# Attention kernel on one core: another table of steps, and the second fill of ones and three reads moved in the prologue

## The reference

```python
# layer 0 and 1: group norm, then attention with 8 heads of 16 channels
xn  = group_norm(x); q, k, v = split(xn @ w_qkv)          # per image: 1024 tokens
out = softmax(q k^T / sqrt(16)) v                         # per head, 1024 x 1024
h0  = out @ w_out + b_out + x                             # layer 0
h1  = out @ w_out + b_out + xn                            # layer 1
# layer 2: layer norm, layer 3: group norm; one head of 128 channels
out = softmax(q k^T / sqrt(128)) v @ Wp + bp + x
```

## Time and profile before

| what | value |
|---|---|
| median of three runs | 2097.07 us (2094.5 to 2097.71) |
| profiled execution: time, span | 2098.85 us, 2097.1 us |
| PE busy | 2034.3 us, 97% |
| PE weight loads | 1147.0 us, 55% |
| DVE busy | 1676.5 us, 80% |
| ACT busy | 1490.4 us, 71% |
| POOL busy | 413.9 us, 20% |
| tile maxima on DVE (line 1227) | 2048, 1271.1 us |
| exponentials on ACT (line 1117) | 2048, 1060.4 us |
| values on PE (line 1473) | 3080 products of 512 columns, 2032 of 256 |

### The profile page before, as it was taken

One profiled execution on the slowest core, in us unless ns is written; L12 is line 12 of the kernel. 1 busy time (PEld: TensorE's weight loads), 2 busy tenths in 40 slices (PEclk: granted clock), 3 DMA queues, 4 the chain that ended last, 5 costly groups with the idle time before them and its releaser, 6 DMA issues.

```text
span 2097.1 us, 40849 instructions
## 1 busy us (share of the span) xinstructions
PE 2034.3 (97%) x15800; PEld 1147.0 (55%) x15800; DVE 1676.5 (80%) x3104; ACT 1490.4 (71%) x2722; POOL 413.9 (20%) x544
## 2 busy tenths in 40 slices
PE   4799999999999999999999999999999999999999
PEld 3344444444744468444873448644585446846988
DVE  6799999999799978898789876898878977773433
ACT  1387788888588854988569874698747986597555
POOL 5002021220122311113120221203111031031231
PEclk7799999999999999999999999999999999999999
DMA  5401351412041314031230502305031040000000
GB/s 148 92 12 40 74 102 31 83 55 49 29 84 39 65 31 81 12 77 27 56 67 2 102 2 57 66 2 102 2 87 27 2 99 4 7 7 2 11 1 21
DMA packets 48592, 97.42 MB, mean 46 GB/s; under 512 B 7824, under 2 KB 10640, under 8 KB 48272
## 3 DMA queue, kind: packets, MB, share of 16 engines
q1 hardware_dynamic: 48400, 94.81, 21.1%
HBM read 55.98 MB, written 37.75 MB: 45 GB/s over the span
## 4 chain that ended last, share of the span: by engine, by line
PE 82%; DVE 10%; DMA 3%; ACT 2%; issue 2%; SPq 1%; POOL 1%; POOLq 0%; DVEq 0%; ACTq 0%
PE outs L1473 19%; PE banks L1435 14%; PE banks L1448 12%; PE outs L1513 11%; PE banks L1491 9%; DVE part_max L1227 8%; PE banks L1354 7%; PE banks L1360 5%; PE banks L1363 4%; ACT probs L1117 2%; DMA q_stack<-shift_parts 2%; SPq L904 0%; DMA q_scratch<-parts 0%; DVE o_turn L1239 0%; DVE stats L1166 0%
## 5 line engine op out<-in xcount | busy, mean ns | idle before, releaser
L1227 DVE TENSOR_REDUCE part_max<-banks 128x1 f32<-128x512 f32 x2048 | 1271.1, 680 | 166.6 <-PE banks L1435 161.4
L1117 ACT ACTIVATE probs<-banks 128x512 f32<-128x512 f32 x2048 | 1060.4, 611 | 200.0 <-PE banks L1448 172.8
L1473 PE MATMUL outs<-probs,v_heads 128*32 128x512 f32 (+1 forms) x5112 | 563.6, 522 | 0.8
L1435 PE MATMUL banks<-k_stack,q_stack 62*128 62x512 f32 x2048 | 550.9, 443 | 4.0 <-DVE part_max L1227 1.3
L1448 PE MATMUL banks<-q_stack,k_stack 64*128 64x512 f32 x2048 | 519.1, 444 | 21.4 <-DMA q_stack<-shift_parts 20.5
L1435 PEld LDWEIGHTS banks<-k_stack,q_stack 62*128 62x128 f32 x2048 | 257.4, 187 | 282.3 <-DVE part_max L1227 114.9
L1448 PEld LDWEIGHTS banks<-q_stack,k_stack 64*128 64x128 f32 x2048 | 244.0, 186 | 236.5 <-ACT probs L1117 77.2
L1124 ACT ACTIVATE probs<-banks,neg_max 128x1024 f32<-128x1024 f32 x128 | 142.7, 1115 | 220.9 <-DVE neg_max L1259 184.7
L1513 PEld LDWEIGHTS outs<-v_full,probs 128*128 128x128 f32 x2048 | 257.4, 191 | 47.0 <-issue 37.2
L1513 PE MATMUL outs<-v_full,probs 128*128 128x128 f32 x2048 | 276.8, 279 | 0.0
L1259 DVE TENSOR_REDUCE neg_max<-banks 128x1 f32<-128x1024 f32 x128 | 156.3, 1223 | 134.0 <-PE banks L1491 133.0
(11 more groups left out here) (107 smaller groups left out, 1160.3 us busy)
## 6 DMA issues: line engine op xcount, KB each, us to landing
k_scratch<-parts SPq DMA_DIRECT2D x64, 256.0 KB
q_scratch<-parts SPq DMA_DIRECT2D x64, 256.0 KB
k_stack<-k_scratch SPq DMA_DIRECT2D x64, 256.0 KB, 6.9
q_stack<-q_scratch SPq DMA_DIRECT2D x64, 256.0 KB, 8.2
k_stack<-k_scratch SPq DMA_DIRECT2D x64, 128.0 KB, 8.2
q_stack<-q_scratch SPq DMA_DIRECT2D x64, 128.0 KB, 9.7
q_stack<-shift_parts SPq DMA_DIRECT2D x256, 4.0 KB
tmp<-x SPq DMA_DIRECT2D x7, 512.0 KB, 3.3
```

Source lines behind the costliest of these rows:

```text
L1117: nc.scalar.activation(probs[:, plan.prob[u], 2 * n + half, :], banks[:, plan.banks["pair", t][k], :], ACT.Exp, scale=HEAD_SCALE).then_inc ...
L1227: nc.vector.tensor_reduce(part_max[:, r % 2, column:column + 1], bank_of(("tile", r, n)), AX_X, ALU.max, negate=True).then_inc(tile_max, 1)
L1435: nc.tensor.matmul(bank_of(("tile", r, n)), qs[rows, i, a, heads, P * t:P * (t + 1)], ks[rows, i, keys, heads, :], start=True, stop=True). ...
L1473: last = nc.tensor.matmul(outs[2 * HD * n:2 * HD * (n + 1), columns], v_heads[:, i, key, at:at + 2 * HD], probs[:, plan.prob[u], n, column ...
```

## The change

Three edits.

1. `STEPS`, the table behind the first 40 tiles, is another string. Both have the same number of T, P, H, S, R, G and Y. The old one has 385 V and 254 U, the new one 433 V and 158 U, so 48 slots whose values were in halves are now in one. Two V with nothing of TensorE's row work between them stand 7 times in the old and 27 times in the new one. Near its start the new table has groups for two slots: four pairs, all tiles of two slots, then V V. How many tiles stand ahead of a given slot is the same to within ten, mostly to within two.
2. The reads (1,k0), (1,q0) and (1,k1) leave the prologue. They stand behind shift 0, with the items of stage 0: the new table begins with a tile and then three C (the product of q1 of image 1, its write, and read (1,k0)), and only then comes the first pair. The other three reads follow in the fourth to the seventh slot.
3. POOL fills the ones of the second half of `k_stack` behind its split of q0 of image 1 (not of q1 of image 0).

```diff
-    FIRST_STEPS = "C" * 29 + "T" * 8 + "C" * 1 + "T" * 4 + "C" * 2 + "T" * 4 + "C" * 2 + "T" * 4 + "C" * 2 + "T" * 4 + "C" * 1 + "T" * 4 + "C" * 3 + "T" * 8 + "H" * 1 + "T" * 4
+    FIRST_STEPS = "C" * 29 + "T" * 8 + "C" * 1 + "T" * 4 + "C" * 2 + "T" * 4 + "C" * 2 + "T" * 4 + "C" * 2 + "T" * 4 + "C" * 1 + "T" * 12 + "H" * 1 + "T" * 4
     STEPS = (
-        "TPTPTTTPTUTPTU TTPTUTPTU TTPTUTPTU TTPTCUTPTU TTPTCUTPTU HTPTUTPTU TTPTPUTTU TPTPCUTTU CTPTTPTV TPTTPV "
-        "TPTTPTV TPTPUTTU TPTPUTTU HTPPTTV TTPPTUTTTTU TPPUU CTPTTPV TPTTTTPUPTU TPTTTUU PTTPUTPTU TPTTHV TPPTTTTUU "
...
+        "TCCCPTPTTTPTUTPTU TTPTUTPTU TTPTUTPTU TTPTCUTPTU CTPTTTPTTPTTPTHV V CTPTTTPTTPTTPTV V CTPTTPTTPTTPV V "
+        "TPTTPTTPTTPTV V TPTTPTTPTTPHV V TPTTPTTTTV V TPTTPPCPTTTV PTTPTTV TTTPTV PTPTTTV PTTPTTUHTPTU PTTPTTV TPPTV "
...
             if i == 1:
                 self.chain(h(0, 1), 0, i, ["q1"])
                 put(h(0, 2), ("write", 1, SPLIT.index("q1")))
-                put(h(0, 5), ("read", 1, "q1"))
+                put(h(0, 3), ("read", 1, "k0"), ("read", 1, "q0"))
+                put(h(0, 5), ("read", 1, "k1"), ("read", 1, "q1"))
                 self.available[1] = h(0, 1)
...
-        order += [("read", 1, n) for n in ("k0", "q0", "k1")]
         return order + tiles[at:]
...
                     elif name in SPLIT:
                         split(name, layer, i)
-                        if (name, layer, i) == ("q1", 0, 0):
+                        if (name, layer, i) == ("q0", 0, 1):
                             pool.wait_ge(*split_done(name, layer, i))
                             fill_ones(1)
                             pool.wait_ge(ones_ready[1], 2)
```

More of the change, by code:

```diff
@@ new lines @@
+        "CTPTTPTPTTPPUU CTTPPUCCTU TTPTTV TTPUU TTPPTTTPPTTUHTPTTCCU TTTPUU TTCV TPPTTTTV PCPTTCTTCTPCTTV TTPTPV "
+        "TTPTTCCCV TTPPCCCTPTTPTTHV TTPTCTPTTTV TTPPV CCPCCCTCTV TPTTPCV CPPTTTV PTPTTUCTPTTTTPTU V CPTPTTTUHPPTTTTU "
+        "UTTTTTPU TPUPTTTTTU UPTTTPTPU TTPPCV CPTTPV TPPTV TPTPTTTV TPTHV TPPTTTTV PTTPTTV TTPTTV PTTPV CTPTPTV "
+        "PTTTPCV TTPTPV TTTTPV TPPTTPTTHCPPTTV TPTTTTPV V TPTPV PCTTTTV CPTTTCTPTCCCCTPTTTV PTTCPTTTV CTTTTPCCV "
+        "TPCPTTTTV PTTHTTTCCCPCCTPTTV CCPPV PPTTCV PPPCV CCTPTTUTTPCTTU TPTTV TTPTTV PPTTTHPTTPTTCTTTPTTV V "
@@ new lines @@
+        "TPPTCCPTTTTV PTTTCV TCPPTCCTTPPV TCTPTTV PPTTV TPTTTTUHPTU TPPTTCTTTPUTTPU TTPV PCPTTTV V CPTPPTTTTV "
+        "TTTTPCUU TTTPPUCU TTPPTCTTPTCCHUU TTPTTV PTTPV TPTTPV PTTPV CPPTTTPTTPTTV TTTTTTCPV TTUTPTTTU "
+        "CCCCCTPTPCTTTTV CCTPTTHCPTCTCTTPTPV PTTPV CCCPTCPTCTV V CPPTTTV PTPTTTV CPTTPTV TPPTTV CHTPTCPTTTPTV TTPTTV "
+        "PTV TTTPTTTTTTTPPV CTPPTV PPTUU TPTTTTPV PTTPTHPTPTTV TPTTTV PTTPV TPPTV V CPTPTTPTV PCTTPTV PTTPTV TPTTPV "
+        "TTPPCTTPTV PTTPV PTTTTV HSV CTTSR CSCR GGGTTTTTTTGGGR STTTGSGYR SGR SGGGGGTTTTTTTGCCGCR YSGTTTTGCGGCR "
@@ new lines @@
+        "CTTPTTCV TPCPTPTCCCTTPTTV UPTTPU TTPV TTPPCPTTV TTPPV PTTV TTPPTV HSV CSR TTTCR GTTTTTTTGGSGSGSGR "
+        "CTTGGYCSGR GGR STTTTGGCGGTTTTGCCYR SGGSGGCR CGGGTTTTTTTGCYCCR SGSGGGCR GGGTTTGCYR HCSGTTTTGGGCCGGR "
+        "TTTGSGCCYR CSGTTGGR GTTCTTGR GSGGYSGCTTGR GGTTTTPGGGGYR PTTGGGGTTTTGGCPTTGGCYTTPTTV PTPTV HPTTUTTTTPCCU "
+        "TPTTPV TPTTPV PPTTTCCCTPTPTTTV TTPPV V PCTTPTUU PTTPV PTTPUTTPCU TPTUHPTTPU TTTPTV PTTTCTPTV PPTPV V "
+        "CPCTTPTV TPPTTV CPTTPTV CPTTPTV TPTTCPV TPTPTV PTTTPV TPTTTHPV CPPTTTUPU TTPTTUU TPTPV TPTTPV CPPTTTV "
@@ new lines @@
+        "CTPTPV TPPTTTTV PTTPV PCTTCTTPTHCPTTTPV PTTTTCCV PTTPV CTCPPTTV CCCTTTPTCV PTCPTCV CCCTCCPTTPV TPTPTUTPU "
+        "PCTTPV CPTTPTV CHPTTTTV CTPPCV CTPPTTTV PTTTTPPV PUU TTTTTTTPPV CPTTPV TPPV TTPPCV TPTPTV CPTTCV "
+        "HPPTTTCCTTTPPV TPPTTV CTTTTPCV CPTTTPCCCPTTPV TTPTV PTTPV TTPTTV CTPTPV TPPTV PTTTV TTPSUU CHSR SCTR "
+        "GGTTTTTGSGSGR CGTTGGYSGR CGTTTTGR GSGCGTTTTGGCR YSGCGGGCTTTTTTGCGR SGGCR YCCGTTTTTTGGSGSCGR GGGCYR "
+        "CTTTTTGGGHSGCSGCR GGGCCYCR TTSCGTTTTTGGGGGR R GGYTTTTSGSCGGTTGR TPTGGGGR YPGGGCTTTTGGGPTTGGYTTTPTCV PTTPTV "
@@ new lines @@
+        "GTTTTTTTGGSGSGSGR GGYR R TTGSGGCGGSGTTTTGCGCYR TTTTGGSGGCCGTTTTGGR SGCCCR YGGGSCTTTTGCGGR TTTTGGCHYR "
+        "SGGCSGGCR CSGTTTTTGGGCCYCR R SGTTTTTGGGGSGSGGYCCR TTTGGR GGTTTTPGGGGYCTTR TTPGGGGGGTPTTTGCGYPTTPTV PTTPV "
+        "TTTPTCHCTPTTTCV PTTPCV TPTTPV PTTPV TPTTTV PPTTTTV TPTPCCPTTV TPTPV TPTPCV PTTTTV HPTTV PTTCTTTPPCV PTTPV "
+        "TPTTPV PCTTPTV TPTPV CTPTTPV TPTTPV TPTTPV CTPPTTV TPPTTTTUPTCTU TTPPV CHPTTTV PTTPV TPTPTV CPTTPV "
+        "PTTPCUTPTPTU TPTTPTTV PTTPV V PCTTCTPTTTCPTTTV PTTTTUPTTCU CTTCPCV HTTPPCCPTTPV PCPTTCCCCCV CCCPTPTV V "
@@ L204 @@
+        "SGGGGR YSGGGGR SGGGGR YSGGGGR SGGGGR YSGGGGR GGGGR YGGGGGGGGY "
     )
```

83 lines of the change are left out of this document (28 added, 55 removed).

## The result

The changed kernel takes 2111.08 us (median of 6 runs, 2105.62 to 2114.82) against 2095.11 us for the kernel before on the same chip: ratio 1.0075 [1.0056, 1.0094]. It is 16 us slower; 20 us faster were forecast. Its profiled execution took 2114.82 us, span 2113.0.

What follows compares the result with a forecast made beforehand. TensorE was taken as the bound, except VectorE between 130 and 530 us. Terms 11.5 + 3 + 3.6 + 2 = 20.1 us off the profiled 2098.85 gave 2078.7; as that execution stood 1.8 above the median, 2077, range 2062 to 2092.

Steps and rivals of the forecast that it cites:

- The prologue: Start of the kernel: with fill and reads moved, pair 0 starts at 67.5 us, 11.5 us gained, bounds 7.6 and 12.
- the first tile: Prologue, first half: first score tile ready at 39.3 us instead of 43.62, with the fill moved away from DVE's copies.
- The lower bound, 71.4: Prologue: pair 0 starts at 71.4 us if the first tile is not earlier, 7.6 us gained.
- the fill's 4.3: Prologue, first half: moving POOL's fill of ones frees DVE's blocked copies, 4.3 us gained, bounds 0 and 5.8.
- the order's rest: Prologue, second half: shift 0 issued ahead of three reads lands sooner; 7.6 us gained if the first tile is not earlier.
- Rivals B: Moved reads delay shift 1, up to 5 us lost, 2082 us; counted inside the main forecast's 0.66.
- C: Prologue: the moved fill blocks DVE's reduces, gain 11.5 - 7.1, 2084 us; chance 0.13 shared with A at half price.
- the table in the DVE stretch: Stages 0 to 3: 360 changes of PE's kind of work become 325; 3 us gained, bounds -3 and 10.
- the PE stretch: Stages 4 to 15: 1084 changes become 1067, at 0.21 us each; 3.6 us gained, bounds 0 and 8.
- Rival A: Table: bunched tiles starve PE of banks, 2105 us at 1.5 us each; chance 0.07 near no difference, 0.05 slower.
- rival D: Table: groups stand only five times, the rest a new fine order; if its waits are better, 2067 us; chance 0.09.
- Two stalls on a shift: Near 1206.84 and 1459 us PE waits for a shift behind reads; 2 us gained, bounds -2 and 6.

Runs made afterwards that it cites:

- e14: New prologue with old table, with GpSimd's fill of the stacks put back to its old place ahead of the first tiles: 2087.12 us, ratio 0.9963.
- e17: The kernel before with the fill's move alone, keeping the old order of first steps, old reads and old table: 2095.86 us, ratio 1.0000.
- e11: The changed kernel with exponentials (from slot 6 on) and tile maxima on 256 of 512 columns, part of the computation left out: 2051.23 us, ratio 0.9789.
- e3: The changed kernel with the new table only up to the first pair of slot 24, old table from there: 2090.84 us, ratio 0.9979.
- e5: e3 with the first of the two values items in each of five groups moved forward to the group's middle: 2085.58 us, ratio 0.9951.
- e18: New prologue, old table with 173 values items moved forward by rule, exponentials and tile maxima on 256 of 512 columns: 2084.10 us, ratio 0.9940.
- e1: The changed kernel's prologue with the table of the kernel before, three C ahead of its first pair: 2081.47 us, ratio 0.9931.
- e15: e1 with the planner's lines on three reads put back to the prologue's end; the issue order stayed as without the edit: 2081.47 us, ratio 0.9935.

## Why the prediction was wrong

**The prologue: right, and its size too.** 11.5 us were forecast; pair 0 gained 11.7, and the first tile came at 40.61 for 39.3 (39.47 in the kernel with the new prologue alone). The lower bound, 71.4 without an earlier tile, is what e14 measured (70.8). It was wrong only to speak of the fill's 4.3 and the order's rest as terms of a sum: the fill's alone is 0 (e17), because what ended last was SP's queue. Rivals B and C fell: the shift of round 1 did not wait for the moved reads, and the maxima beside the fill stayed at 0.60 us. The sum took the fill to cost nothing in its new place; no row of before shows a fill beside maxima, and what shows it is this run.

**The step that failed: the table in the DVE stretch and in the PE stretch, +3 and +3.6 us, in fact -13.0 and about -16.** Both terms priced a change of PE's kind of work and took it that PE's own time, where PE is busy 97%, comes out at the end. The changes may save something, 3.8 us outside the shift stretches, seen only where drains are cheap (e11). With the drains as they are, PE, DVE and ACT turn round seven banks, and in the groups looked at the time is the work of a drain plus what it idles under values. There more products between two values items meant both a wait for banks and a longer idle time: 0.7 us for a group where PE is busy, 0.9 where DVE is the bound, about 1 in rounds 0 and 1 (5 us for five, by e3 and e5).

**Rival A was the nearest, and had 5% as slower and 7% as no difference.** It named banks and gave 2105; measured 2111. That it came so close is in part luck: it charged 1.5 us to each of 19 additional stretches with many tiles, and the runs found the cost in values done in one go behind more products, of whatever kind, than there are banks. Against it I put that the tiles by slot are unchanged and DVE has time in hand. Both are true and beside the point: time in hand wasn't kept. DVE stood idle 196.8 us ahead of its maxima with the new table and 160.9 with the old one (rows below), and the run took 30 us longer. That an engine which idles can't work it off later, with seven banks ahead of it, is my reading of this, and no run shows it by itself. Its sign was also too narrow. The waits of the tiles' weight loads for maxima, whose sum I named, hardly moved (114.9 and 114.1 after). Those of the pairs' weight loads rose, here with the new prologue alone, then after (us in total, times, longest):

```profile
PEld banks L1447 <- DVE part_max L1226: 78.1, 128, 1.7
```

```profile
PEld banks L1447 <- DVE part_max L1226: 92.3, 157, 1.3
```

With the tiles' waits for exponentials (91.8 and 100.0) and the pairs' (76.7 and 76.0), weight loads waited 364 us for the two drains and 382 after, 18 us more. The drains themselves, in the same two kernels:

```profile
L1226 DVE TENSOR_REDUCE part_max<-banks 128x1 f32<-128x512 f32 x2048 | 1270.9, 680 | 160.9 <-PE banks L1434 155.8
L1116 ACT ACTIVATE probs<-banks 128x512 f32<-128x512 f32 x2048 | 1060.0, 610 | 187.0 <-PE banks L1447 160.5 <-PE outs L1512 14.0 <-PE outs L1472 0.3
```

```profile
L1226 DVE TENSOR_REDUCE part_max<-banks 128x1 f32<-128x512 f32 x2048 | 1269.8, 678 | 196.8 <-PE banks L1434 192.1
L1116 ACT ACTIVATE probs<-banks 128x512 f32<-128x512 f32 x2048 | 1055.8, 615 | 220.7 <-PE banks L1447 196.4 <-PE outs L1512 15.2 <-PE outs L1472 1.1
```

35.9 and 33.7 us more of idle time, at nearly unchanged work, for 30 us of run time. As the work is unchanged, the idle time has to rise by about the run time whatever the cause: these rows say where DVE and ACT stood still, and what shows the cause are the runs with groups and with cheap drains. With the change known as groups of two slots (rival D counted them, five), I set the other fifteen doubled values that the new table has more of (27 - 7 - 5) and the longer stretches at nothing.

**Two stalls on a shift, +2 us: the stalls went, the time did not.** In rounds 41 to 44 and 49 to 52 PE idles 7.9 us before and 3.2 after, but those stretches are 1.9 and 2.0 us longer, and over all six shift stretches PE idles 12.0 us after, 10.7 before. A part that no step had stands there: 23.8 us at the lower clock against 10.2 before and 6.8 with the prologue alone. The window behind round 42 of the changed kernel, and the one behind the stall of the earlier trace rows before:

```profile
1225.00:1245.00 20.00, 20.00 (x136) 8.20 (x140) 14.44 (x28) 16.16 (x33) 7.18 (x13) 0.83 0.00 1
```

```profile
1207.00:1229.00 22.00, 22.00 (x155) 8.48 (x156) 16.73 (x31) 18.62 (x36) 7.79 (x14) 0.92 0.01 1
```

In the shift stretches together the three kernels that have the new table from slot 24 on show 17.0 to 23.8 us of it, the ten that have the old one in most of them 3.4 to 13.6 us, and the one with the late groups 0 (with cheap drains 20.4). So in these traces it goes with the table, but not place by place: in rounds 49 to 52 the three show 6.8, 6.8 and 0 us. Here it is worth 8.5 us of the 30, in the average of the executions about 6 for the whole kernel. Which waits bring it about was not settled: in rounds 41 to 44 PE idled 2.3 us with the new table and 4.6 before, and the clock was low for longer with less idle time.

What stays open besides: half of what the values cost when they come early (e18), and the 3.5 us of work that the new table has more in the shift stretches (a balance: once idle time and half of the low clock are off, rounds 58 to 61 take 3.3 us less with it, 41 to 44 and 49 to 52 some 2.4 us more each).

## What to carry to other kernels

When an engine is 97% busy and hands its results through a few buffers, price a new order by what it does to the engines that empty them: count the products between two items that fill no buffer against the number of buffers. The producer's summed waits say little (they rose by 2 us where 33 were lost, and by 18 where 30 were), and the drains' idle time only says where they stood still; a run with cheap drains says whether they are the cause. Of the orders tried here the old, even one was the best; values later in bunches and values earlier both lost. Of two edits on one path, measure each alone: the fill was worth 0 or 4.6 us, by whether the queue behind it was free.

## What the runs showed of the hardware

Beside a memset of GpSimd on SBUF (27.84 to 34.94 us), two of VectorE's four SBUF copies took 3.61 and 3.55 us and ended within 0.15 us of the memset's end; the other two took 0.2. In the changed kernel, with no memset beside them, all four took 0.22 us. VectorE's reduces from PSUM were not held up there: the 11 that ran wholly beside the 7.07 us of fill took 674 to 676 ns each, the 18 ahead of it 674 to 690, and all 32 went through at 0.60 us from one to the next.

In these traces a stall on TensorE could cost twice. Before, PE stood still for 2.0, 3.6 and 2.3 us ahead of the first pairs of rounds 6, 42 and 50, and each time 3.4 us at a granted clock of 0.50 followed. It is not so every time: in the changed kernel 1.9 us of idling at round 34 were followed by none, and 6.8 us in rounds 42 and 49 came where PE had not stood still for 1 us at a time. At 0.50 the 16 values products of a group took 3.64 us (groups with cheap drains, at 1422.48 us), at 1.00 they took 1.92. The time of a shift stretch was that of the undisturbed one plus the wait plus half of the low time: with these two taken off, the six shift stretches come to 737.3, 737.3, 737.5, 737.3 and 736.4 us in the five kernels of the old table that differ in the prologue alone (before, e1, e14, e15, e17), while the raw sums lie between 748.9 and 756.7.
